# A decoder layer on one core: values of the cross-attention turned by VectorE blocks and small DMAs, and five of eight query tiles moved into the next group

## What is computed

```python
x = layernorm(x + mixer_block(x))                 # a state-space mixer and an MLP
xn = layer_norm(x, ln_g, ln_b); cn = layer_norm(context, cln_g, cln_b)
q = (xn @ Wq) in 16 heads of 64, scaled by 1/8    # per sequence 112 x 16 rows
k, v = split(cn @ Wkv)                            # one key and one value head for all: 375 x 64 each
attn = softmax(q @ k.T + mask)                    # 375 context rows
out = (attn @ v) @ Wout + (silu(xn @ W1_gate) * (xn @ W1_value)) @ W2
x = layernorm(x + out)
x = layernorm(x + fp8_quantized_ffn(x))
```

## Time and profile before

| | |
|---|---|
| median of three runs | 1870.61 us (1868.58 to 1872.76) |
| profiled execution | 1873.19 us |
| its span | 1871.40 us |
| TensorE busy | 1785.0 us, 95% of the span |
| VectorE, ScalarE, GpSimd busy | 1307.4, 924.6, 417.9 us (70%, 49%, 22%) |
| mean granted TensorE clock | 0.978 of full speed |
| DMA moved | 106 MB, 57 GB/s over the span |

### The profile page before, as it was taken

The page is one execution under the profiler, slowest core; times in us unless marked ns, Lnnn a source line. Parts: engine busy times, 40 slices in busy tenths (PEclk is TensorE's granted clock), DMA queues, the critical chain, the costliest instruction groups (busy, mean ns, idle before and its releaser), DMA issues.

```text
span 1871.4 us, 27865 instructions
## 1 busy us (share of the span) xinstructions
PE 1785.0 (95%) x9320; PEld 1037.1 (55%) x9320; DVE 1307.4 (70%) x3970; ACT 924.6 (49%) x2262; POOL 417.9 (22%) x569
## 2 busy tenths in 40 slices
PE   4579999999999999999999999999999999999997
PEld 2446766766767544455545555545555554555466
DVE  6888988988967587376567657657747656765744
ACT  3344553563441465456445455545644654654542
POOL 4867776876871000000000000000000000000000
PEclk8589999999999999999999999999999999999999
DMA  4000001001013252123222232223222322222200
GB/s 131 11 11 11 21 21 30 11 21 31 1 39 131 74 154 77 50 76 73 62 64 71 60 80 62 60 67 80 59 64 73 75 64 64 67 64 71 54 13 20
DMA packets 75182, 106.15 MB, mean 57 GB/s; under 512 B 11456, under 2 KB 68736, under 8 KB 74144
## 3 DMA queue, kind: packets, MB, share of 16 engines
q1 hardware_dynamic: 74576, 103.90, 20.9%
q10 hardware_dynamic: 464, 0.46, 0.1%
HBM read 96.92 MB, written 7.42 MB: 56 GB/s over the span
## 4 chain that ended last, share of the span: by engine, by line
PE 77%; DVE 15%; DMA 3%; issue 2%; ACT 1%; POOL 1%; SPq 0%; DVEq 0%; POOLq 0%; ACTq 0%
PE ps L1515 20%; PE ps L1470 9%; PE ps L1477 9%; PE ps L1508 9%; PE ps L1493 8%; DVE m_u L727 3%; PE ps L387 3%; PE ps L405 3%; PE ps L314 3%; DVE m_rs L759 2%; PE ps L1575 2%; PE ps L373 2%; PE ps L440 1%; PE ps L1569 1%; DMA m_Rd<-bc_roots 1%
## 5 line engine op out<-in xcount | busy, mean ns | idle before, releaser
L1858 DVE CUSTOM_DVE_ANT_0 x_pr<-ps,x_mk 128x375 f32<-128x375 f32 x448 | 227.8, 546 | 299.8 <-issue 174.8
L1730 ACT ACTIVATE x_pT<-ps 125x384 f32<-125x384 f32 x448 | 195.4, 489 | 252.9 <-PE ps L1477 252.0
L1736 ACT ACTIVATE x_pr<-x_pr,x_mx 128x375 f32<-128x375 f32 x448 | 268.2, 608 | 31.8 <-DVE x_mx L1858 31.7
L1477 PEld LDWEIGHTS ps<-ident,x_pr 128*125 128x125 f32 x1344 | 164.6, 187 | 130.0 <-issue 94.5
L1515 PE MATMUL ps<-x_xn,x_w 128*128 128x448 f32 x512 | 206.6, 545 | 1.6 <-DVE x_ff L1918 1.6
L1477 PE MATMUL ps<-ident,x_pr 128*125 128x128 f32 x1344 | 205.8, 289 | 2.0 <-DVE x_pr L1867 2.0
L1470 PE MATMUL ps<-x_kT,x_qT 64*128 64x375 f32 x896 | 202.6, 528 | 4.6 <-DVE x_mx L1858 3.6
L1867 DVE TENSOR_SCALAR x_pr<-x_pr,x_rc 128x375 f32<-128x375 f32 x448 | 170.3, 423 | 8.0
L1493 PE MATMUL ps<-x_pT,x_va 125*64 125x512 f32 (+1 forms) x768 | 158.4, 548 | 0.6 <-ACT x_pT L1730 0.6
L314 PE MATMUL ps<-m_xa,w_in 128*128 128x448 f32 x352 | 147.9, 567 | 6.2 <-ACT m_xa L532 6.2
L1470 PEld LDWEIGHTS ps<-x_kT,x_qT 64*128 64x128 f32 x896 | 68.2, 185 | 123.3 <-issue 109.4
(11 more groups left out here) (196 smaller groups left out, 2897.3 us busy)
## 6 DMA issues: line engine op xcount, KB each, us to landing
x_mk<-in_mask SPq DMA_DIRECT2D x224, 187.5 KB, 2.4
x_cx<-in_context SPq DMA_DIRECT2D x32, 375.0 KB
x_cT<-in_context_turned SPq DMA_DIRECT2D x32, 375.0 KB, 3.3
x_rb<-context_roots SPq DMA_DIRECT2D x32, 187.5 KB, 5.4
m_Rd<-bc_roots SPq DMA_DIRECT2D x8, 448.0 KB, 3.6
x_mixed<-m_x SPq DMA_DIRECT2D x8, 448.0 KB, 3.8
X<-x_mixed SPq DMA_DIRECT2D x8, 448.0 KB, 4.3
m_X<-in_x SPq DMA_DIRECT2D x7, 448.0 KB, 3.9
```

Of the source, the lines that this page charges most:

```text
L1477: last = pe.transpose(bank(2 + e)[0:JP, t * ROWS:(t + 1) * ROWS], pr[:, 2 * (p % SLOT) + e, t * JP:(t + 1) * JP], ident[:, :])
L1730: act.activation(pT[:, 2 * NV * (batch(p) % 2) + 2 * (p % NP % NV) + e, :, :].rearrange("p t s -> p (t s)"), bank(2 + e)[0:JP, 0:JT * ROWS ...
L1736: act.activation(pr[:, k, :], pr[:, k, :], ACT.Exp, scale=-1.0, bias=mx[:, k:k + 1], accum_out=sums[:, k:k + 1]).then_inc(h_e.sem, 1)
L1858: dve.tensor_tensor_reduce(pr[:, k + e, :], bank(e)[:, 0:J], mk[:, p % SLOT, :], -1.0, 3.0e38, ALU.add, ALU.min, mx[:, k + e:k + e + 1]).t ...
```

## The change

The piece `vback` disappears. Instead VectorE, in the piece `kv`, writes the values into the lower half of a wider `vT` (three parts of 125 columns, each in a row of 128, the last three columns zero), waits for that write and for the DMAs of the values before, and transposes the 64 x 384 floats in blocks of 32 x 32 into the upper half. SP, in step r = 6 after that step's mask (and once ahead of group 0), waits for the transpose and issues eight DMAs (`VPARTS` = 8), each of which moves a block row of up to 32 partitions with three runs of 32 floats to its place in `va`. `times_v` waits for those DMAs. Of the query tiles, numbers 0 to 2 stay in step 27 and numbers 3 to 7 go to slot X of steps 0 to 4 of the next group, ahead of the `out` pieces there; `scores` waits for tiles 0 and 1 at step 0 and for tile p + 1 at steps 1 to 6. Opening and first group keep all eight tiles in the opening; the last group computes its tiles 3 to 7 itself. The diff, with few of its unchanged lines:

```diff
--- before.py
+++ after.py
@@ -1054,6 +1054,7 @@
 CONTEXT = (0, 1, 4)
+VPARTS = DH // 32 * (ROWS // 32)
@@ -1080,9 +1081,10 @@
     for b in range(GB):
-        for r, kind in ((NP - 2, "kv"), (NP - 1, "vback")):
-            at[(b - 1) % GB * NP + r, "X"].insert(0, (kind, b))
-    at[STEPS - 1, "Y"] += [("query", n) for n in range(KA)]
+        at[(b - 1) % GB * NP + NP - 2, "X"].insert(0, ("kv", b))
+    at[STEPS - 1, "Y"] += [("query", n) for n in range(QUERIES)]
+    for n in range(QUERIES, KA):
+        at[n - QUERIES, "X"].append(("query", n))
@@ -1097,15 +1099,16 @@
 W1_AT = 10
+QUERIES = 3
 START = [("token", 0), ("token", 1), ("mlp", 0), ("mlp", 1), ("query", 0), ("mlp", 2), ("query", 1), ("mlp", 3), ("query", 2),
-         ("mlp", 4), ("query", 3), ("mlp", 5), ("query", 4), ("mlp", 6), ("kv", 0), ("query", 5), ("mlp", 7), ("query", 6), ("vback", 0),
-         ("query", 7)]
-AHEAD = [piece for piece in START if piece[0] != "mlp"]
+         ("mlp", 4), ("query", 3), ("mlp", 5), ("query", 4), ("mlp", 6), ("kv", 0), ("query", 5), ("mlp", 7), ("query", 6), ("query", 7)]
+STARTED = [piece for piece in START if piece[0] != "mlp"]
+AHEAD = [piece for piece in STARTED if piece[0] != "query" or piece[1] < QUERIES]
 BEHIND = ([("out", c, n) for c in range(KD) for n in range(4)] + [("back", 0), ("back", 1), ("ftoken", 0), ("ftoken", 1)]
-          + [("up", n) for n in range(KH)] + [("down", 0), ("down", 1)])
+          + [("up", n) for n in range(KH)] + [("down", 0), ("down", 1)] + [("query", n) for n in range(QUERIES, KA)])
@@ -1114,8 +1117,8 @@
         return 2
-    if piece[0] in ("kv", "vback"):
-        return 2 if piece[1] != 1 else int(piece[0] == "vback")
+    if piece[0] == "kv":
+        return 2 if piece[1] != 1 else 0
@@ -1125,8 +1128,8 @@
         body, opening = ([x for p in range(STEPS) for s in "XY" for x in at[p, s] if x[0] != "out" or x[2] == 3] for at in (AT, AT_FIRST))
-        self.start, _ = self.places(AHEAD)
-        self.first, n0 = self.places([("start",) + x for x in AHEAD] + [x for x in opening if x not in BEHIND])
+        self.start, _ = self.places(STARTED)
+        self.first, n0 = self.places([("start",) + x for x in STARTED] + [x for x in opening if x not in BEHIND])
@@ -1201,7 +1204,7 @@
     kT = sb("x_kT", [128, 2, J])
-    vT = sb("x_vT", [128, J])
+    vT = sb("x_vT", [128, JT, ROWS])
@@ -1241,6 +1244,8 @@
     l_ct = count("x_lct", 16 * GB)
+    l_va = [count(f"x_lva{n}", VPARTS * 16 * GB // 2) for n in range(2)]
+    c_t = count("c_t", GB)
@@ -1371,6 +1376,14 @@
+        def values_in(i, b):
+            sp.wait_ge(c_t.sem, c_t.value(i, b + 1))
+            hold(sp, h_o, i, NB * (b - 1))
+            for k in range(DH // 32):
+                for q in range(ROWS // 32):
+                    n = min(32, JP - 32 * q)
+                    sp.dma_start(va[32 * q:32 * q + n, b % 2, :, 32 * k:32 * k + 32], vT[32 * k:32 * k + n, :, 32 * q:32 * q + 32]).then_inc(l_va[b % 2].sem, 16)
+
@@ -1415,6 +1428,8 @@
                     roots_in(g, n)
+                if r == NP - 1:
+                    values_in(g, n)
@@ -1441,6 +1456,7 @@
         tokens_out(LAST - 2)
+        values_in(0, 0)
@@ -1459,9 +1475,8 @@
             b, r = divmod(p, NP)
-            if p == 0:
-                for n in (KA - 2, KA - 1):
-                    emptied(pe, i - 1, ("query", n))
+            for n in range(2) if p == 0 else (p + 1,) if p < NP else ():
+                emptied(pe, i - 1 if n < QUERIES or i == 0 else i, ("query", n))
@@ -1483,7 +1498,7 @@
             if r == NV - 1:
-                emptied(pe, made_in(i, b), ("vback", b))
+                pe.wait_ge(l_va[b % 2].sem, l_va[b % 2].value(i, VPARTS * 16 * (b // 2 + 1)))
@@ -1574,12 +1589,6 @@
                 last.then_inc(done, 1)
-            elif kind == "vback":
-                pe.wait_ge(c_v.sem, c_v.value(held_by(it, n), n + 1))
-                to, done = vacant(pe, it, piece)
-                for t in range(JT):
-                    last = pe.transpose(to[0:JP, t * DH:(t + 1) * DH], vT[DH:2 * DH, t * JP:(t + 1) * JP], ident[DH:2 * DH, DH:2 * DH])
-                last.then_inc(done, 1)
@@ -1596,7 +1605,7 @@
                     if p == MLP_DOWN[2]:
-                        emptied(pe, -1, ("vback", 0))
+                        emptied(pe, -1, ("kv", 0))
@@ -1605,7 +1614,7 @@
                 emptied(pe, NG - 1, ("value", KH - 1))
-                emptied(pe, NG - 1, ("vback", 3))
+                emptied(pe, NG - 1, ("kv", 3))
@@ -1922,13 +1931,13 @@
                 src, _ = filled(dve, it, piece)
-                if it >= 0:
-                    filled(dve, it if n != 1 else it - 1, ("vback", (n - 1) % GB))
-                dve.tensor_scalar(vT[DH:2 * DH, :], src[DH:2 * DH, 0:J], kvb[DH:2 * DH, :], None, ALU.add).then_inc(c_v.sem, 1)
-            elif kind == "vback":
-                src, done = filled(dve, it, piece)
-                hold(dve, h_o, held_by(it, n), NB * (n - 1))
-                dve.tensor_copy(va[:, n % 2, :, :], src[0:JP, 0:JT * DH].rearrange("p (t d) -> p t d", d=DH)).then_inc(done, 1)
+                dve.tensor_scalar(vT[DH:2 * DH, :, 0:JP], src[DH:2 * DH, 0:J].rearrange("p (t q) -> p t q", q=JP), kvb[DH:2 * DH, :], None, ALU.add).then_inc(c_v.sem, 1)
+                dve.wait_ge(c_v.sem, c_v.value(held_by(it, n), n + 1))
+                last = n - 1 if n > 0 else GB - 1
+                if held_by(it, n) > 0 or n > 0:
+                    at = held_by(it, n) if n > 0 else held_by(it, n) - 1
+                    dve.wait_ge(l_va[last % 2].sem, l_va[last % 2].value(at, VPARTS * 16 * (last // 2 + 1)))
+                dve.transpose(vT[0:DH, :, :].rearrange("p t q -> p (t q)"), vT[DH:2 * DH, :, :].rearrange("p t q -> p (t q)")).then_inc(c_t.sem, 1)
@@ -2010,6 +2019,7 @@
+        dve.memset(vT[DH:2 * DH, :, JP:ROWS], 0.0)
@@ -2025,7 +2035,6 @@
         context_norm(0, 1, 0)
-        part(-1, ("vback", 0))
```

## The result

The changed kernel takes 1848.92 us in the median of four runs (1846.68 to 1851.38), beside 1869.80 us for the kernel before in the same comparison: 20.9 us less. The ratio is 0.9886, 95% interval 0.9868 to 0.9905. The profiled execution took 1850.02 us with a span of 1848.10.

What follows compares the result with a forecast made beforehand. TensorE's own work, full from 800 to 1750 us, was taken as the bound. Removing "vback" gave 31 x 0.66 + 0.1 = 20.6 us, the other parts nothing: 1870.61 - 20.6 = 1850.0 us, range 1846.4 to 1857.5.

Steps and rivals of the forecast that it cites:

- Part 1: On TensorE, removing the values' way back ("vback") saves 0.66 us in 31 contexts plus 0.1, 20.6 us.
- Rival (a): On TensorE only the transposes' own 0.47 us goes per context: 14.6 us saved, 1856.0 us; chance 0.12.
- Step 6: In group 0, where TensorE waits for VectorE anyway, removing "vback" is worth 0 to 0.66 us, taken as 0.1.
- Rival (c): In group 0, 3.6 us of waits coinciding with GpSimd's scaling shift against VectorE and vanish: 1846.4 us; chance 0.05.
- Part 2: VectorE loses a 0.36 us copy and gains a transpose of 0.45 us (423 ns to about 1.7 us), covered outside group 0.
- The cover of step 12: Tightest place for VectorE's added work, with some 4 us of cover less the 0.66 that TensorE comes earlier.
- Part 3: On SP's queue, eight DMA issues per context take 4.4 to 8.2 us, taken as 4.4, and cost nothing.
- My serial reading of the fixed cost: About 2.0 us per DMA read as queue price: 16 us for eight, 2.2 over the spare, 1918 us.
- rival (d): SP's queue passes the eight transfers one after another at 2.4 us each: 167 us lost, 2017 us; chance 0.04.
- My 13.8 us of cover: Spare on SP's queue before the next mask is late: wanted after 16.2 us, of which landing takes 2.4.
- Part 4: Five query tiles move from step 27 (7.5 us less) to steps 0 to 4 (1.5 us more each): worth 0.
- rival (b): The moved query tiles pay a hand-over of 0.19 us each on TensorE: 6.7 us given back, 1856.7 us; chance 0.06.

Runs made afterwards that it cites:

- the runs with six and with one: Kernel before with each context's three TensorE value transposes made twice: ratio 1.0047; with only one of the three made: 0.9967.
- the queries alone: Kernel before with only the five query tiles moved and the scores' waits on single tiles: ratio 0.9989.
- the values alone: Changed kernel with all eight query tiles back in step 27 (QUERIES = 8): 1851.10 us, ratio 0.9884.
- the run with five transposes: Changed kernel with four more VectorE transposes of the same block per context, each waiting for the one before: 1857.79 us, ratio 0.9936.
- the kernel with ten transposes: Changed kernel with nine more VectorE transposes of the same block per context, each waiting for the one before: 1926.94 us in one execution.

## Why the prediction was right, and where its steps were off

The forecast was 1850.0 us, 20.6 under before; measured were 1848.92 and 20.9. The main step held exactly: TensorE bounds from 759 us on, "vback" is worth 0.66 us from scores to scores, and it is gone in 31 of 32 places.

**Part 1** was right in size and wrong in its inner division. The 0.47 us from the first transpose to the next tile was taken as the transposes' own; the runs with six and with one show 0.32. It did no harm because all edges left together. Rival (a), built on that division, did not come about: step 13 is at 7.42, not 7.6.

**Not in the sum**: the wait for the eighth query tile. The border held it, 0.84 us from the turn of the earlier trace rows at 1063.28 to the scores at 1064.12 (0.75 with the queries alone), and the opening had 0.84 us of it behind L1759; I looked at neither as a wait. It gave 0.9 us in the opening and 0.1 at each border, 1.5 us by the run with the queries alone.

**Group 0** was mis-sized the other way, 1.10 us instead of 2.08. Step 6 gave nothing (6.53 us for steps 6 and 7 before, 6.58 after), for which 0.1 stood. The larger part is in steps 18 and 19, 1.33 us longer, around the stop by GpSimd. TensorE's two waits there are 4.6 us instead of 3.6, and the rest is work at the low clock behind them; the stop itself is 5.1 us instead of 4.5 (5.85 and 5.26 less the usual 0.74). GpSimd's halving began 8.2 us after the first of the weights was issued, 7.4 us in the kernel before. Whether the change has to do with that stays open: the two steps together took 15.4 us with the queries alone and with the DMAs on GpSimd's queue, 12.5 with the values alone, 14.0 and 14.6 in the kernels with six and with one transpose, so they vary by more than the 1.3, each in a single trace. Rival (c) had the right place, but nothing removed the stop until ScalarE took the work. These two misses, +1.5 and -1.0, nearly cancel, and that is why the total fits within 0.4 us: that closeness is luck.

**Part 2**: the transpose takes 0.573 us, not 0.45, and nothing came of it. The cover was named wrongly: not step 12 is the tightest place but step 27, with 1.5 us by the run with five transposes, because I asked when TensorE's scores want the maxima and not when ScalarE's queue does. The cover of step 12, some 3.4 us as reckoned, was nearly right: with 5.5 us more on VectorE TensorE waited 2.57 us there. What the sums of a lost cover left out is the lower clock behind a wait. The Trainium skill's figure ("VectorE: DVE Perf Modes", section "The three transpose paths"), 0.93 us by the estimate from it, was for another type and is over the measured 0.573.

**Part 3**: 5.32 us for eight issues, within 4.4 to 8.2, and free, as the run over GpSimd's queue shows. That it lies within was luck: the 0.55 and 1.03 us from which I made the ends were unusually long issues, the medians in the kernel before are 0.33 us for a mask and 0.43 for a turned context, and ends made from those, 2.6 and 3.4, would have missed. My serial reading of the fixed cost in the Trainium skill ("DMA: Bandwidth & Descriptors", section "Anatomy of one DMA"), 16 us for eight, is refuted by 5.32; rival (d) did not come about. My 13.8 us of cover hold in groups 2 to 6 (16 us of queue were still free there), but not in the first, where steps are short and the roots come first.

**Part 4**: the moved tiles cost nothing and bring nothing, steps 0 to 4 are longer by 1.50 us each, rival (b) did not come about.

## What to carry to other kernels

Where one engine is full, price a piece by the distance between the same two instructions in a step with it and in one without it: that gave 0.66 us, which neither the durations (3 x 0.27) nor the gap (0.47) would have. To price the cover of an added instruction, ask which queue behind it is first to stand, not which wait the full engine shows; and take the cover from the stretch with the shortest steps. And a wait of an otherwise full engine can cost more than itself: behind several of its waits here TensorE worked on at a lower clock for some microseconds, so that a stop with 4.6 us of waits cost 7.7. The move of work within the full stretch was worth nothing by itself.

## What the runs showed of the hardware

- Fp32 transposes of 64x64 operands on TensorE cost 0.107 us each and 0.34 us per visit between 128-row work, measured with one, three and six of them (7.86, 8.08 and 8.40 us for the step), at a granted clock of 1.00 there.
- In the changed kernel TensorE worked only 0.6 us between 697.6 and 702.8 us, and its granted clock was 0.50 from about 701.5 to 708.2 us; four matmuls of 448 columns took 3.36 us there and 1.67 elsewhere. The same shows behind waits of 2.57 us (0.53 in the 3.3 us after it) and 3.71 us (0.62 in the 3.8 us after it) in the kernel with ten transposes, and not behind one of 0.68 us (1.00) in the kernel with five.
- A VectorE block transpose of 64 x 384 float32 takes 0.573 us, beside 0.42 for an elementwise pass of 128 x 375.
- SP needs 0.63 us to issue an SBUF-to-SBUF DMA of 96 runs of 128 bytes, more than for a mask of 128 runs of 1500 bytes (0.33); GpSimd's queue shows a median of 0.55 for the same DMA, but a mean of 0.77 and 6.14 us for eight of them, against SP's 5.32.
- GpSimd's multiplication of 128 x 2048 floats in SBUF (5.4 us) stopped VectorE for 3.3 to 5.1 us in nine traces, in a division in seven of them and in a 112 x 4 row of a root's iteration in two; ScalarE did the same multiplication in 1.91 us without a stop.
